# Graph layer on one core: the edge stage's update rectified in transposed form

## The reference

```python
h = relu(layernorm(x))                                 # x: (50000, 128)
em = concat([h[src], h[dst]])                          # (25000, 256)
em = relu(layer_norm(em @ msg_w + msg_b) * msg_g + msg_beta) * edge_weights
messages = segment_sum(em, dst) / counts               # 0 where a node has no edge
gate = sigmoid(h @ gate_w + gate_b)
u = layer_norm(concat([h, messages]) @ upd_w + upd_b) * upd_g + upd_beta
out = x + gate * relu(u) + (1 - gate) * h
```

## Time and profile before

| what | value |
|---|---|
| runs | 1055.12, 1056.28, 1071.27 us; median 1056.28 |
| profiled execution | 1053.59 us, its span 1052.1 us |
| mean granted clock of PE | 0.834 of 2.4 GHz |
| busy share of the span | DVE 79%, ACT 77%, PE 69%, POOL 58% |
| scatters and gathers on POOL | 1.0 us each |

### The profile page before, as it was taken

One profiled execution on the slowest core, in us unless ns is written; L12 is line 12 of the kernel. 1 busy time (PEld: TensorE's weight loads), 2 busy tenths in 40 slices (PEclk: granted clock), 3 DMA queues, 4 the chain that ended last, 5 costly groups with the idle time before them and its releaser, 6 DMA issues.

```text
span 1052.1 us, 20637 instructions
## 1 busy us (share of the span) xinstructions
PE 729.7 (69%) x4448; PEld 588.4 (56%) x4448; DVE 833.7 (79%) x3740; ACT 811.5 (77%) x3396; POOL 605.7 (58%) x602
## 2 busy tenths in 40 slices
PE   2377686776767677777666547777777778778772
PEld 2256565654545556555545336666665667667661
DVE  7287888886877888778789347999999988888984
ACT  2378787877868788778779258999999977878973
POOL 5555555554545555555555746666666666665557
PEclk9787978887888887788776668999989888988986
DMA  5255655565655666566532211322221121111110
GB/s 147 76 177 175 209 182 190 187 200 179 196 173 192 215 198 199 171 200 206 192 117 68 90 38 62 95 92 83 94 89 54 62 70 54 61 63 58 65 67 34
DMA packets 74548, 133.66 MB, mean 127 GB/s; under 512 B 16134, under 2 KB 18006, under 8 KB 74482
## 3 DMA queue, kind: packets, MB, share of 16 engines
q1 hardware_dynamic: 53868, 97.58, 27.1%
q0 software_dynamic: 18912, 34.84, 11.8%
q10 hardware_dynamic: 1702, 0.53, 0.2%
HBM read 56.01 MB, written 80.81 MB: 130 GB/s over the span
## 4 chain that ended last, share of the span: by engine, by line
ACT 47%; PE 16%; another core or an unknown queue 15%; issue 11%; DVE 7%; POOL 3%; ACTq 1%; DMA 0%; DVEq 0%; POOLq 0%; SPq 0%
ACT hrow L406 14%; ACT junk L413 13%; ACT xload L406 4%; ACT work L444 3%; PE py L1290 3%; POOL out L626 3%; PE pt L1248 3%; ACT lnv L388 2%; PE pm L1313 2%; ACT work L1159 2%; PE pm L1315 2%; ACT rs L393 2%; ACT at L1099 1%; PE py L1254 1%
## 5 line engine op out<-in xcount | busy, mean ns | idle before, releaser
L626 POOL DMA_INDIRECT out<-work,sidx x196 | 202.7, 1034 | 135.3 <-issue 54.2
L413 ACT ACTIVATE junk<-py 128x128 bf16<-128x128 f32 x588 | 155.7, 292 | 74.8 <-remote 64.2
L621 POOL DMA_INDIRECT ring<-in_x,gidx x140 | 141.9, 1013 | 89.7 <-DVE work L465 47.4
L406 ACT ACTIVATE hrow<-xload,nb,rs 128x128 f32<-128x128 f32 x392 | 163.9, 525 | 1.6 <-issue 0.8
L621 POOL DMA_INDIRECT ring<-in_x,src_i x116 | 116.3, 1002 | 68.4 <-issue 31.5
L1290 PE MATMUL py<-w_u,work 128*128 128x129 f32 x784 | 144.9, 341 | 0.0
L1290 PEld LDWEIGHTS py<-w_u,work 128*128 128x128 f32 x784 | 122.7, 238 | 28.2 <-issue 28.2
L413 ACT ACTIVATION_READ_ACCUMULATOR junk<-py 128x1 f32 x588 | 130.7, 223 | 0.0
L1254 PE MATMUL py<-bias,ones 3*128 3x258 bf16 x294 | 66.8, 313 | 77.6 <-ACT work L1099 56.8
L621 POOL DMA_INDIRECT work<-in_x,gidx x56 | 55.8, 996 | 108.9 <-DVE work L465 97.9
L1248 PE MATMUL pm<-ident,work 128*128 128x128 f32 x376 | 72.4, 325 | 63.4 <-ACT work L1104 31.9
(11 more groups left out here) (179 smaller groups left out, 2049.0 us busy)
## 6 DMA issues: line engine op xcount, KB each, us to landing
xload<-in_x SPq DMA_DIRECT2D x98, 256.0 KB
normalised_rows<-hrow SPq DMA_DIRECT2D x98, 256.0 KB
out<-work SPq DMA_DIRECT2D x98, 256.0 KB
running_sums<-acc SPq DMA_DIRECT2D x49, 256.0 KB
staged_target_rows<-work SPq DMA_DIRECT2D x14, 256.0 KB
ring<-staged_target_rows SPq DMA_DIRECT2D x14, 256.0 KB, 2.8
out<-work,sidx POOLq DMA_INDIRECT x196
ring<-in_x,gidx POOLq DMA_INDIRECT x140
```

The source lines that it names most:

```text
L406: last = nc.scalar.activation(dest[:, m, :], rows[:, m, :], ACT.Relu, bias=nb[:, s4, at + m:at + m + 1], scale=rs[:, s4, at + m:at + m + 1])
L413: last = nc.scalar.activation(junk[:, j, k, :], prod[:, k, 0:H], ACT.Square, scale=scale, accum_out=mv[:, slot, at + k, 1:2])
L621: pool.indirect_dma_start(out=dest, out_offset=None, in_=rows, in_offset=bass.IndirectOffsetOnAxis(ap=idx, axis=0), **({} if rows is sums_ ...
L626: pool.indirect_dma_start(out=out, out_offset=bass.IndirectOffsetOnAxis(ap=idx, axis=0), in_=rows, in_offset=None, **if_tail).then_inc(s, 16)
```

## The change

The edge stage's update is rectified as the node stage's is. DVE scales `py` by `rs` in one instruction (`scaled`). PE flips the result into `pt[:, 0]`, which ACT has emptied of flipped source rows. ACT rectifies it with gain and shift as columns. PE flips it back into `pa`, which ACT has emptied of flipped sums. DVE multiplies by the gate and adds the mix (`gated_sum`). With it go the separate shift, the four gated rectifications on ACT and the last addition on DVE. The final rows of group s-7 are done in step s, not s+1, so DVE's steps are one fewer. The part that mixed rows early in the drain is gone; the weighting of messages stands behind the mixing; ACT empties `pa` after the squares and the turned rectification, not before. The helpers `scaled`, `gated_sum` and `turned_relu` are shared with the node stage, whose instructions stay as they are.

```diff
-        ed = stages("edge", {**common, "stats": 4, "h": 2, "ht": 1, "flip": 2,
+        ed = stages("edge", {**common, "turned": 1, "back": 1, "stats": 4, "h": 2, "ht": 1, "flip": 2,
...
+        def scaled(dve, d, g, slot, at):
+
+            one_mark(d["gamma"], dve, g, nc.vector.tensor_tensor(
+                t_buf[:, g.at % 4], py[:, g.at % 2, :, 0:H],
+                rs[:, slot, at:at + G].unsqueeze(2).to_broadcast([P, G, H]), ALU.mult))
+
+        def gated_sum(dve, d, f, prod):
+
+            d["mix"].after(dve, f)
+            d["back"].after(dve, f)
+            for k in range(G):
+                last = nc.vector.scalar_tensor_tensor(o[:, f.at % 4, k, :], prod[:, k, :], gt[:, f.at % 4, k:k + 1],
+                                                      o[:, f.at % 4, k, :], ALU.mult, ALU.add)
+            one_mark(d["final"], dve, f, last)
...
-                drained = fin and s.at >= EG
-                if drained:
-                    ed["rest"].after(dve, g)
-                    dve.wait_ge(s_scat[g.at % 4], g.rounds(16 * G))
-                if s.at == EG:
-                    early = mix_early(2)
-                f = s.back(8)
-                if live(f, EG):
-                    final(dve, nc.vector, ed, f, o[:, f.at % 4])
-                if drained and s.at <= EG + 2:
-                    early = mix_early(early + 1)
...
+                if fin:
+                    ed["rstd"].after(dve, s)
+                    scaled(dve, ed, g, s.at % 4, 3 * G)
                 q = s.back(3)
...
-                if fin:
-                    ed["rstd"].after(dve, s)
-                    one_mark(ed["gamma"], dve, g, by_std(t_buf[:, g.at % 4], py[:, g.at % 2], s.at % 4, 3 * G, g_upd))
-                    beta(dve, ed, g, t_buf[:, g.at % 4], be_upd)
...
                 if new:
                     L.wait()
                     moment(L, s, 2 * G, 2)
+                if fin:
+                    gated_sum(dve, ed, g, rows4(pa[:, :]))
...
-            straight_steps(edge_step, EG, 8, 6, tail_step)
+            straight_steps(edge_step, EG, 7, 6, tail_step)
...
+                if live(s.back(6), EG):
+                    post(act, ed, s.back(6), (s.at + 1) % 4, 3 * G, G, 1.0)
+                if live(s.back(7), EG):
+                    turned_relu(ed, s.back(7), pt[:, 0, :])
                 g = s.back(5)
                 if live(g, EG):
                     evacuate(ed, g, at_[:, g.at % 2, :], pa[:, :], ACT.Copy, "at", "aflip")
-                if live(s.back(6), EG):
-                    post(act, ed, s.back(6), (s.at + 1) % 4, 3 * G, G, 1.0)
...
-                if live(s.back(7), EG):
-                    ed["gate"].after(act, s.back(7))
-                    gated_relu(act, ed, s.back(7))
...
                     ed["sum"].after(pe, g)
+                    if beyond(g, 3):
+                        ed["final"].after(pe, g.back(3))
                     one_mark(ed["aflip"], pe, g, flip(pa[:, :], acc[:, g.at % 4]))
+                u = s.back(7)
+                if live(u, EG):
+                    ed["gamma"].after(pe, u)
+                    if live(s.back(2), EG):
+                        ed["ht"].after(pe, s.back(2))
+                    one_mark(ed["turned"], pe, u, flip(pt[:, 0, :], t_buf[:, u.at % 4]))
                 g = s.back(2)
...
                     one_mark(ed["msg"], pe, g, last)
+                if live(u, EG):
+                    ed["relu"].after(pe, u)
+                    if live(s.back(5), EG):
+                        ed["at"].after(pe, s.back(5))
+                    elif beyond(u, 1):
+                        ed["final"].after(pe, u.back(1))
+                    one_mark(ed["back"], pe, u, flip(pa[:, :], t_buf[:, u.at % 4]))
```

More of the change, by code:

```diff
@@ L772, in node_sum @@
                 if live(f, NG) and turned(f):
-                    nd["mix"].after(dve, f)
-                    nd["back"].after(dve, f)
-                    for k in range(G):
-                        last = nc.vector.scalar_tensor_tensor(o[:, f.at % 4, k, :], pm[:, k, :], gt[:, f.at % 4, k:k + 1],
-                                                              o[:, f.at % 4, k, :], ALU.mult, ALU.add)
-                    one_mark(nd["final"], dve, f, last)
+                    gated_sum(dve, nd, f, pm)
                 elif live(f, NG):
@@ L962, in edge_step @@
                     L.mark(row_stats(L, s, slot(s, 1), G))
-                if live(q, EG):
-                    weights = cont_wb[:, q.at * 2 * G + G:(q.at + 1) * 2 * G]
-                    ed["gamma_m"].after(dve, q)
-                    one_mark(ed["msgw"], dve, q, nc.vector.scalar_tensor_tensor(
-                        acc[:, q.at % 4], acc[:, q.at % 4], 0.0, weights.unsqueeze(2).to_broadcast([P, G, H]),
-                        ALU.max, ALU.mult))
                 if node is not None:
                     node_sum(node)
-                if fin and not drained:
+                if fin:
                     ed["rest"].after(dve, g)
@@ L988, in edge_step @@
                         before = acc[:, m.at % 4, k, :]
-                    if fin and k >= early:
+                    if fin:
                         last = mix_row(g, k, h_dst[:, (g.at + NG) % XS], slot(g, 1), o[:, g.at % 4])
@@ L995, in edge_step @@
                     one_mark(ed["mix"], dve, g, last)
+                if live(q, EG):
+                    weights = cont_wb[:, q.at * 2 * G + G:(q.at + 1) * 2 * G]
+                    ed["gamma_m"].after(dve, q)
+                    one_mark(ed["msgw"], dve, q, nc.vector.scalar_tensor_tensor(
+                        acc[:, q.at % 4], acc[:, q.at % 4], 0.0, weights.unsqueeze(2).to_broadcast([P, G, H]),
+                        ALU.max, ALU.mult))
                 if new:
@@ L1099, in evacuate, with turned_relu @@
                 one_mark(d[stage], act, g, nc.scalar.activation(dest, source, func))
-            def turned_relu(r):
-                nd["turned"].after(act, r)
-                one_mark(nd["relu"], act, r, nc.scalar.activation(
-                    t_buf[:, r.at % 4].rearrange("p k h -> p (k h)"), pa[:, :], ACT.Relu, bias=shift_col[:, :],
+            def turned_relu(d, r, source):
+                d["turned"].after(act, r)
+                one_mark(d["relu"], act, r, nc.scalar.activation(
+                    t_buf[:, r.at % 4].rearrange("p k h -> p (k h)"), source, ACT.Relu, bias=shift_col[:, :],
                     scale=gain_col[:, :]))
@@ L1114, in node_step @@
                 if live(s.back(5), NG):
-                    turned_relu(s.back(5))
+                    turned_relu(nd, s.back(5), pa[:, :])
                 rstds(act, nd, s, 2 * G)
```

11 lines of the change are left out of this document (2 added, 9 removed).

## The result

The changed kernel took **1095.18 us** (median of 4 runs, 1090.19 to 1097.67), the kernel before beside it 1055.7 us (4 runs, 1051.74 to 1071.27): **1.038 times as long, 95% interval 1.033 to 1.044**. Forecast were 1043 us and a range of 1023 to 1074, so the sign was wrong too. A later repeat on another chip gave 1.025 (1.017 to 1.033). The profiled execution of the changed kernel took 1095.5 us, its span is 1093.8 us.

The account below looks back on a forecast made before the run. The prediction took ACT to bound early edge steps, with PE late at times. First 20 steps -5, next 14 -8, last five +1, drain -1: -13 on 1053.59 us profiled, the runs' median 2.7 higher, so 1043 us, range 1023 to 1074.

Parts of the forecast that it names:

- The bound: Early edge steps: ACT sets the step, 8.64 us before and 8.35 after, with PE late only in some steps.
- 1.0 us of slack for PE: Early edge steps: PE's flip is ready 1.0 us before ACT wants it; after the change 0.15 us is left.
- As many low stretches cost 11.7, none 0, I take a little over half: First 20 counted steps: low clock's cost lies between 11.7 us and none; a little over half makes the stretch 5 less.
- PE's loop: Later edge steps: PE's round per step grows from 6.68 by 0.43 and 0.43 to 7.54 us and becomes the bound.
- A third of the low clock's loss stays, since PE's products stand closer together.: Next 14 steps: a third of 2.23 us lost per step remains; 8.3 us per step, 8 us less in all.
- I cost this wait at nothing: Edge steps on DVE: gated sums' wait for PE's flip back costs nothing, that flip being due before the update product.
- The wait of the sums' flip for the final sum three groups back costs nothing: Edge steps on PE: this wait costs nothing, since DVE ends a step before PE's last flip.
- Edits costed at nothing: Reordering on DVE and ACT: pm free 0.61 us later, within slack; sums' evacuation moved behind, counted only on ACT.
- A drain step is a longer chain now, up to 2 later: Drain: POOL's stream starts up to 2 us earlier, the longer chain up to 2 later; -1 us taken.
- Last five steps: Last five counted edge steps: between 7.54 and 8.54 us each, -0.5 to +4.5 us in all; +1 taken.
- (b): Rival, edge steps: PE takes ACT's place at today's low clock; 0 + 12 + 4.5, +16, 1073 us; chance 0.1.
- (c): Rival, edge steps: transposes bring more low clock, 10.3 us per step, +59, 1115 us; chance 0.13.

Follow-up runs that it names:

- e1: Kernel before plus eight transposes of the identity per edge step on PE, read by nobody and with no added wait: 1.005 of the kernel before.
- e4: Changed kernel, with the flip of the scaled rows waiting only for the evacuation of the first half of pt: 1.011 of the kernel before.
- g1: e9 with the evacuation of the sums ahead of the squares in every step: 1.002 of the kernel before.
- e8: e4 with the last six groups also going the way of the kernel before, without turned flips: 1.008 of the kernel before.
- e3: Changed kernel, with ACT's order in the last six steps: sums' evacuation, turned rectification, then squares: 1.027 of the kernel before.
- e10: Changed kernel, with the gated sum reading unturned rectified rows from SBUF, not waiting for the flip back, which stays on PE unread: 1.028 of the kernel before.
- e11: Changed kernel, both new flips turning the identity unread, rectification and gated sum reading SBUF: 1.020 of the kernel before.
- f1: Kernel before, with scaling and shift of the update product moved ahead of the message normalisation on DVE: 1.028 of the kernel before.
- h1: e11 with the message normalisation ahead of the scaling on DVE: 1.020 of the kernel before.
- h2: e11 with the evacuation of the turned sums ahead of squares and rectification on ACT: 1.010 of the kernel before.
- e9: e8 with ACT's order of the kernel before restored in the last six steps: 1.003 of the kernel before.

## Why the prediction was wrong

**The bound** was the failing step. The prediction had ACT at the end of an early step, with PE late now and then, and counted 1.0 us of slack for PE. ACT's part was right: an undisturbed early step was forecast at 8.35 and measures 8.15 us,

```profile
705.65 0.58 ACT L1148 ACTIVATE work<-pt 128x512 f32<-128x512 f32 x1
...
713.80 0.58 ACT L1148 ACTIVATE work<-pt 128x512 f32<-128x512 f32 x1
```

8.64 before; the wait of the turned rectification is 6.6 us in 360 in all, near the 0.2 per step. But only three of 20 steps in the changed kernel were below 8.35, and the mean is 9.61. The slack was taken from one good step. In the mean, leg b is 6.0 us and leg c 2.1, where the prediction had 5.5 and 1.08 from rows at the high clock, and with leg a 0.65 to 0.8 us longer the step grew by 0.5 to 0.6: a slack of 1.0 would have swallowed it. The step that the slack was read from had none. ACT was to want the second half at 718.54, with the flip's result there since 717.53; the next row of that timeline of the kernel before has ACT idle and the evacuation 0.70 us late:

```profile
719.24 0.60 ACT L1159 ACTIVATE work<-pt 128x512 f32<-128x512 f32 x1 [0.60 <-remote]
```

Nine of those 20 steps were longer than 8.7 us; the six of the earlier trace rows are only the waits named "remote". "As many low stretches cost 11.7, none 0, I take a little over half" was a choice with no row behind it. Result -5 forecast, +12.7 measured; for the next 14 steps -8 forecast, +5.1 measured. For the steps ahead of the 20 and the one between the stretches the sum had no term: +3.0 us each.

**PE's loop.** Base 6.68, plus 0.43, plus 0.43. The second increment was right (leg b, 0.2 to 0.5). The first was too small: leg a grew by 0.65 to 0.8 and not 0.43, and in e1, where the transposes wait for nothing more, by 0.59 in a clean step (0.65 to 1.24). The base was the value of a step at full clock, 2.2 us below the mean.

**"A third of the low clock's loss stays, since PE's products stand closer together."** Refuted for the change as it was: 9.28 us per later step, forecast 8.3, at a clock of 0.89 (0.88 before). The gap of which the argument spoke did not shrink: legs c and a together are 3.1 to 3.2 us in the later steps, 2.9 to 3.0 before. Its idea stays open. For it: e4 and g1, where transposes fill the gap, had 0.96 and 0.98 in the first stretch. Against it: e8 with the same flip had 0.94 there, as had e3, e10 and e11 without it; and f1, with c and a together 3.35 us, had 0.85, the changed kernel's repeat with 3.32 had 0.92. Also, "the steps with a late flip are those of low clock" was misread. In the kernel before, the four later steps with a c of about 4 us (3.98 to 4.06) ran at a granted clock of 0.99 or 1.00, and the step behind each at 0.63 or 0.79; the repeat has four more such pairs. There the low clock follows the late flip. As to the rule of the Trainium skill ("TensorE: Matmul & The Clock Gate", Part 4: PE-mode transpose), by which transposes earn no clock: e1, with eight more and no shorter gap in legs a and c, had 0.90 in the first stretch, as the repeat of the kernel before. In the later stretch it had 0.95, the kernel before 0.88 twice, which speaks against the rule, by one profile. They cost no clock; whether they earn any no run here shows apart from the gap.

**DVE.** "I cost this wait at nothing": the wait was there, 78 us, and by e10 its cost is nothing that can be measured. The number was right, its reason (the flip back is done by then) wrong. The item in the list of signs, "wrong if DVE waits for the flip back", would have been no proof. "The wait of the sums' flip for the final sum three groups back costs nothing" did not hold as a wait: PE stood 5.3 us before it in four steps. What that cost no run shows apart.

**Edits costed at nothing.** The move of the scaling ahead of the message normalisation was priced as 0.61 us later for pm, in slack; with the short scaling that held (h1), with the old long one it costs 2.8% (f1). The move of the sums' evacuation behind squares and rectification was counted only for ACT's own row of work, not for who waits for it: 3.7 to 6.3 us of drain (h2 against e11 and h1). That is the second step that failed; whether the place costs anything ahead of the drain is not shown.

**Drain.** Forecast -1, measured +10.3. "A drain step is a longer chain now, up to 2 later" priced the chain once. It is a ring, gone through in each of the last steps, since on PE the flip back stands ahead of the update product, and on ACT the scale behind the tail's evacuation. With the last six groups not turned and ACT's old order there (e9, g1) it is 47.0 and 47.9 us.

**Last five steps:** +1 forecast, +0.7 measured. **Rivals:** the outcome is (b), "PE takes ACT's place with the low clock of today", with chance 0.1 and a price of 16 us; it should have been the forecast, since in the mean PE's slack was already used up. That its three terms (0, 12 and 4.5) add up nearly to the 18.5 measured in the three stretches is luck: they measured 12.7, 5.1 and 0.7. The drain and the steps around were not in it. (c) did not happen: the clock did not fall.

**Open:** why the single step between the two long stretches takes 10.2 to 10.7 us in the changed kernel and in e11, and 7.4 before; why the loss is 3.8% beside one chip's runs and 2.5% beside another's; and why e3 spent 16 to 20 us less than the changed kernel on the same instructions ahead of the drain.

## What to carry to other kernels

When steps alternate between good and late ones, take the slack from the mean round of each engine, leg by leg, over the whole stretch, and not from the best step; here the mean named PE where the best step and the busy shares named ACT. A short operation put into an engine that works in order can cost more than its length if others wait behind it: let it wait for exactly the buffer that it writes, and put it into a gap that is there anyway (17.7 us in the medians, on each of two chips, 1.6 to 1.9% of the kernel, hung on one semaphore). And an evacuation that is moved behind other work is to be costed for the engine that waits for it, in the drain above all, where each step is a ring of such waits.

## What the runs showed of the hardware

By the code the evacuation of the second half waits for nothing but PE's last pt flip. In the kernel before it comes 0.64 us after the record of that flip's start at the least, 1.08 us in the clean step of the earlier trace rows and 3.98 us in the next, of which ACT stands idle for 2.35, put down to "remote". So records of PE can stand ahead of what it does, and a loop summed from the records alone is too short. The mean of leg c cannot be read so in the early steps, where ACT itself comes 2.10 us after the flip without ever being idle. In the changed kernel the flip at 694.71 was evacuated 1.84 us later, at high clock:

```profile
696.55 0.60 ACT L1150 ACTIVATE work<-pt 128x512 f32<-128x512 f32 x1 [0.81 <-PE pt L1238]
```

The node steps, the same in all kernels, ended between 557.3 and 585.6 us, by chip and execution; the stage after them repeated within 0.4 us in the kernel before, and differed by 16 to 20 us between e3 and the changed kernel on the same instructions.
